# Casts of a pair's split on ScalarE instead of VectorE, and a reordered start, in a one-core recommendation tower

## What is computed

```python
e = stack([tbl_f[ids[:, f]] for f in range(39)], axis=1)      # x0: 512 x 39 x 16
xk = x0 = e
for W in (f0, f1, f2):                                         # 39*39, 128*39, 128*39 rows x 128
    z = einsum('bfd,bgd->bfgd', x0, xk).reshape(b, f * g, d)
    xk = einsum('bpd,pm->bmd', z, W);  outs.append(xk)
h = concatenate([concatenate(outs, 1).sum(-1), dense_ctx], 1)
h = maximum(h @ W_top1 + b1, 0);  h = maximum(h @ W_top2 + b2, 0);  y = h @ W_top3
```

## Time and profile before

| | |
|---|---|
| median of 3 runs | 708.94 us (708.28 to 708.96) |
| profiled execution: its own time | 706.03 us |
| its span, first to last instruction | 704.3 us |
| busy: PE, DVE, ACT, POOL | 96%, 88%, 71%, 36% of the span |
| chain that ended last | PE 60%, DVE 19%, issue 8%, ACT 3% |

### The profile page before, as it was taken

The page is one execution under the profiler, slowest core; times in us unless marked ns, Lnnn a source line. Parts: engine busy times, 40 slices in busy tenths (PEclk is TensorE's granted clock), DMA queues, the critical chain, the costliest instruction groups (busy, mean ns, idle before and its releaser), DMA issues.

```text
span 704.3 us, 11656 instructions
## 1 busy us (share of the span) xinstructions
PE 673.9 (96%) x3569; PEld 489.3 (69%) x3569; DVE 616.7 (88%) x1412; ACT 498.5 (71%) x1663; POOL 254.7 (36%) x247
## 2 busy tenths in 40 slices
PE   3787999999999999999999999999999999999998
PEld 0365677667777887767777778666776787777777
DVE  1579899999999877999999887899999887899991
ACT  3156678778786657878786657778787666787882
POOL 5674817148512707126710713406831000111020
PEclk9799999999999999999999999999999999999999
DMA  7630121203020210202111020110302020030000
GB/s 227 229 80 23 36 62 22 74 3 96 4 82 11 51 47 4 82 12 63 39 49 42 15 84 4 48 46 22 78 11 83 1 66 28 0 92 1 1 1 2
DMA packets 23411, 33.85 MB, mean 48 GB/s; under 512 B 7815, under 2 KB 10615, under 8 KB 22966
## 3 DMA queue, kind: packets, MB, share of 16 engines
q1 hardware_dynamic: 18230, 31.84, 14.7%
q0 software_dynamic: 5120, 1.29, 2.0%
HBM read 9.13 MB, written 0.00 MB: 13 GB/s over the span
## 4 chain that ended last, share of the span: by engine, by line
PE 60%; DVE 19%; issue 8%; ACT 3%; DMA 0%; SPq 0%; DVEq 0%
DVE sums L684 9%; PE x_ps L921 9%; PE v_ps L777 8%; PE v_ps L779 6%; PE v_ps L778 6%; PE a_ps L777 6%; PE a_ps L779 6%; PE a_ps L778 6%; PE s_ps L891 4%; PE s_ps L980 3%; ACT scaled L451 2%; DVE scaled L627 2%; DVE sums L673 1%; DVE scaled L617 1%; DVE z_sb L657 1%
## 5 line engine op out<-in xcount | busy, mean ns | idle before, releaser
L451 ACT ACTIVATE scaled<-a_ps,x0c 128x128 f32<-128x128 f32 x1216 | 350.3, 379 | 132.6 <-PE a_ps L779 125.7
L684 DVE SCALAR_TENSOR_TENSOR sums<-v_ps,x0c,sums 128x128 f32<-128x128 f32 x768 | 214.9, 340 | 33.3 <-PE v_ps L779 33.2
L777 PE MATMUL v_ps<-w_hi,x_hi 128*128 128x512 f32 x320 | 175.9, 550 | 8.5 <-DVE e_parts L573 4.5
L393 POOL DMA_INDIRECT e_sb<-in_tables,ids_now x140 | 165.5, 1182 | 41.1 <-issue 39.2
L409 POOL TENSOR_TENSOR diag_sb<-x0c,eye_sb 128x320 f32<-128x320 f32 x64 | 61.1, 955 | 316.4 <-PE s_ps L980 316.1
L779 PE MATMUL v_ps<-w_hi,x_lo 128*128 128x512 f32 x320 | 127.0, 397 | 0.0
L778 PE MATMUL v_ps<-w_lo,x_hi 128*128 128x512 f32 x320 | 126.5, 395 | 0.0
L777 PE MATMUL a_ps<-w_hi,x_hi 128*128 128x512 f32 (+1 forms) x320 | 124.2, 388 | 0.0
L779 PE MATMUL a_ps<-w_hi,x_lo 128*128 128x512 f32 (+1 forms) x320 | 123.1, 385 | 0.0
L778 PE MATMUL a_ps<-w_lo,x_hi 128*128 128x512 f32 (+1 forms) x320 | 123.1, 385 | 0.0
L921 PE MATMUL x_ps<-z_sb,w_sb 117*128 117x512 f32 (+1 forms) x210 | 108.0, 595 | 0.5 <-DVE z_sb L657 0.5
(11 more groups left out here) (112 smaller groups left out, 635.7 us busy)
## 6 DMA issues: line engine op xcount, KB each, us to landing
b_sb<-a_sb SPq DMA_DIRECT2D x300, 78.0 KB
w_sb<-in_w SPq DMA_DIRECT2D x1, 2496.0 KB
e_sb<-in_tables,ids_now POOLq DMA_INDIRECT x140, 2.6
s_sb<-in_w SPq DMA_DIRECT2D x2, 1024.0 KB, 5.1
wt_sb<-in_wt SPq DMA_DIRECT2D x1, 768.0 KB
s_sb<-in_w SPq DMA_DIRECT2D x1, 512.0 KB, 9.9
wt_sb<-in_wt SPq DMA_DIRECT2D x1, 512.0 KB
w_raw<-in_w0a SPq DMA_DIRECT2D x1, 409.5 KB
```

The costliest lines, as they stand in the source:

```text
L393: pool.indirect_dma_start(out=e_sb[0:rows, i, :], out_offset=None, in_=tables, in_offset=bass.IndirectOffsetOnAxis(ap=ids_now[0:rows, 0, i ...
L451: last = nc.scalar.activation(scaled[:, s % 2, to, j, :], bank[:, j * MAPS:(j + 1) * MAPS], ACT.Copy, scale=x0c[:, k % 4, s, lo + j:lo + j ...
L684: nc.vector.scalar_tensor_tensor(out=sums[:, s % 2, j, :], in0=v_ps[n % 2][:, j * MAPS:(j + 1) * MAPS], scalar=x0c[:, k % 4, s, lo + j:lo ...
L777: nc.tensor.matmul(to, high, w_high, start=True, stop=False)
```

## The change

- The two casts of a pair's split (pairs 1 to 7) go from DVE to ACT (`cast_pair`, at the head of ACT's half, at the first and third place of `split_at`); the two subtractions stay on DVE. Chunk 0's four places are 10, 11, 13, 14, where they were 11, 12, 13, 14.
- W1: its third piece is loaded ahead of W0 and all ids; the second piece is turned into four other banks; all three pieces are turned, rounded and subtracted ahead of x0.
- Filler matmuls of 512 columns (`warm_up`), 9, 1, 2 and 3 of them, stand around the turning of chunk 0's x0.
- Gathers: the second ten of the start no longer wait for `x0t`, and pair 1's are no longer paced.
- Chunk 1's first x0 is turned after the first half of chunk 0, and its rows of x0 after the third half; before, both stood ahead of chunk 0. Chunk 0's z0 places are (6, 8, 10, 11, 13, 14, 15), where they were (2, 4, 7, 9, 12, 14, 15), and its x0 turn stands at 16 and 18.
- The first group of each chunk waits for `x1_hi`, and only its third matmul for `x1_lo`; before, the group waited for `x1_lo` at its head.

```diff
-PACED_FROM, PACED_BY = 5, 0.6
+FIRST_TURN_AT, FIRST_A_AT = 0, 2
+FIRST_Z0_AT = (6, 8, 10, 11, 13, 14, 15)
+WARM_UPS = (9, 1, 2, 3)
-FIRST_SPLIT_AT = (11, 12, 13, 14)
-X0_TURN_AT = (15, 17)
+FIRST_SPLIT_AT = (10, 11, 13, 14)
+X0_TURN_AT, FIRST_X0_TURN_AT = (15, 17), (16, 18)
-        w1_banks = v_ps + a_ps
+        w1_banks = [v_ps + a_ps, [pair_ps, x1_ps, turn_ps, s_ps], v_ps + a_ps]
...
             for n in range(2):
-                if n == 1:
-                    pool.wait_ge(x0t_ready, 1)
                 for i in range(FQ):
...
-                if isinstance(pair, int) and pair == 1 and step > PACED_FROM:
-                    pool.wait_ge(v_done, 1 + int(PACED_BY * (step - 1 - PACED_FROM)))
...
+            def cast_pair(pair, step):
+                if step == 0:
+                    act.wait_ge(e_in, 16 * FH * pair)
+                    act.wait_ge(turned, 2 * pair)
+                    nc.scalar.activation(parts_of(e_parts, 0), e_sb[:, :, :].rearrange("p (u i) d -> p d u i", u=2),
+                                         ACT.Copy).then_inc(e_cast, 1)
+                if step == 2:
+                    act.wait_ge(e_left, pair)
+                    nc.scalar.activation(parts_of(e_parts, 1), e_rest[:, :, :].rearrange("p d (u i) -> p d u i", u=2),
+                                         ACT.Copy).then_inc(e_cast, 1)
...
             def split_pair(pair, step):
-                if step == 0:
-                    dve.wait_ge(e_in, 16 * FH * pair)
-                    dve.wait_ge(turned, 2 * pair)
-                split(step, ...)
+                if step == 1:
+                    dve.wait_ge(e_cast, 2 * pair - 1)
+                    nc.vector.tensor_tensor(rest, whole, parts_of(e_parts, 0), ALU.subtract).then_inc(e_left, 1)
+                if step == 3:
+                    dve.wait_ge(e_cast, 2 * pair)
+                    nc.vector.tensor_tensor(parts_of(e_parts, 2), rest, parts_of(e_parts, 1),
+                                            ALU.subtract).then_inc(e_split, 1)
...
             def first_pairs():
-                low_w1(1)
...
                 split_first(1)
-                low_w1(2)
...
+            def warm_up(n):
+                for _ in range(n):
+                    nc.tensor.matmul(x1_ps[:, :], sel_sb[:, IDB:IDB + 128], sel_sb[:, 0:COLS], start=True, stop=True)
...
+            for p in range(len(W1_PIECES)):
+                turn_w1(p)
             pe.wait_ge(consts_in, 32)
+            pe.wait_ge(w1_lo_ready, 8)
+            warm_up(WARM_UPS[0])
             turn_first(0)
+            warm_up(WARM_UPS[1])
...
                 nc.tensor.matmul(to, high, w_low, start=False, stop=False)
+                if low_ready:
+                    pe.wait_ge(x1_lo_ready, low_ready)
                 return nc.tensor.matmul(to, low, w_high, start=False, stop=True)
...
-                    if k == -1 and h == HALVES - 2:
-                        turn_first(1)
...
                         if h == 0:
-                            pe.wait_ge(x1_lo_ready, 4 * t + k + 1)
+                            pe.wait_ge(x1_hi_ready, 4 * t + k + 1)
...
+                    if 4 * t + k == 0 and h == FIRST_TURN_AT:
+                        turn_first(1)
+                    if 4 * t + k == 0 and h == FIRST_A_AT:
+                        pe.wait_ge(x0t_ready, 2)
+                        rows_of_x0(1)
...
+                warm_up(WARM_UPS[2])
                 pe.wait_ge(a_ready, 1)
                 for i in range(2):
                     select(i)
+                warm_up(WARM_UPS[3])
...
                     if i == T0 - 2:
-                        turn_w1(2)
+                        columns_of_x0(0)
```

More of the change, by code:

```diff
@@ L210, in dlrm_tower @@
         e_in = sem("e_in")
-        e_step = sem("e_step")
+        e_cast = sem("e_cast")
+        e_left = sem("e_left")
         e_split = sem("e_split")
@@ L506, in slot @@
                         nc.scalar.activation(x1_hi[:, (k + 1) % 2, :], x1_ps[:, :], ACT.Copy).then_inc(x1_hi_ready, 1)
-                    if k % 2 == 0 and k > -2 and h - 1 in X0_TURN_AT and exists(t, k + 2):
-                        part = X0_TURN_AT.index(h - 1)
+                    if k % 2 == 0 and k > -2 and h - 1 in x0_turn_at(t, k) and exists(t, k + 2):
+                        part = x0_turn_at(t, k).index(h - 1)
                         act.wait_ge(turned, 4 * t + k + 2 + part + 1)
@@ L581, in split_pair @@
             def split_pair(pair, step):
-                if step == 0:
-                    dve.wait_ge(e_in, 16 * FH * pair)
-                    dve.wait_ge(turned, 2 * pair)
-                split(step, e_sb[:, :, :].rearrange("p (u i) d -> p d u i", u=2),
-                      e_rest[:, :, :].rearrange("p d (u i) -> p d u i", u=2),
-                      lambda part: parts_of(e_parts, part), e_step, 3 * (pair - 1), e_split)
+                whole = e_sb[:, :, :].rearrange("p (u i) d -> p d u i", u=2)
+                rest = e_rest[:, :, :].rearrange("p d (u i) -> p d u i", u=2)
+                if step == 1:
[5 more added lines that the diff above has]
+                                            ALU.subtract).then_inc(e_split, 1)
             def low_w1(p):
@@ L601, in _ @@
             low_w1(0)
+            low_w1(1)
+            low_w1(2)
             dve.wait_ge(pads_ready, 4)
@@ L847, in last_block, with columns_of_x0, rows_of_x0 @@
                     mm.then_inc(y_done, 1)
+            def columns_of_x0(k):
+                for s in range(SUBS):
+                    mm = nc.tensor.matmul(turn_ps[:, F0 * s:F0 * (s + 1)], x0t[:, k % 4, 128 * s:128 * s + 128],
+                                          sel_sb[:, SEL_3:SEL_3 + F0], start=True, stop=True)
+                mm.then_inc(x0c_done, 1)
+            def rows_of_x0(k):
+                nc.tensor.matmul(pair_ps[0:3 * F0, :], sel_a, x0t[:, k % 4, :],
+                                 start=True, stop=True).then_inc(a_done, 1)
             def slot(t, k):
@@ L873, in slot @@
                             pe.wait_ge(y_ready, t)
-                        for s in range(SUBS):
-                            mm = nc.tensor.matmul(turn_ps[:, F0 * s:F0 * (s + 1)],
-                                                  x0t[:, (k + 1) % 4, 128 * s:128 * s + 128],
-                                                  sel_sb[:, SEL_3:SEL_3 + F0], start=True, stop=True)
-                        mm.then_inc(x0c_done, 1)
-                    if h == HALVES - 1 and exists(t, k + 2):
+                        columns_of_x0(k + 1)
+                    if h == HALVES - 1 and k != -1 and exists(t, k + 2):
                         pe.wait_ge(x0t_ready, x0t_events(t, k + 2))
@@ L882, in slot @@
                             pe.wait_ge(h2_ready, tile + 1)
-                        nc.tensor.matmul(pair_ps[0:3 * F0, :], sel_a, x0t[:, (k + 2) % 4, :],
-                                         start=True, stop=True).then_inc(a_done, 1)
+                        rows_of_x0(k + 2)
                     if step is not None and step in OUT2_AT:
@@ L908, in slot @@
                                 pe.wait_ge(macs, mac_count(at, last, 3))
-                        group(v_ps[n % 2], t, k, s, V_FIELDS[i]).then_inc(v_done, 1)
+                        group(v_ps[n % 2], t, k, s, V_FIELDS[i], 4 * t + k + 1 if h == 0 else None).then_inc(v_done, 1)
                         if not isinstance(t, int) or HALVES * 4 * t + n >= 2:
@@ L960, in slot @@
                     if turns_x0:
-                        part = X0_TURN_AT.index(h)
+                        part = x0_turn_at(t, k).index(h)
                         for d in range(D // 2):
```

69 lines of the change are left out of this document (38 added, 31 removed).

## The result

The changed kernel takes 701.99 us (median of 4 runs, 700.05 to 702.32) against 708.61 (4 runs, 707.78 to 708.96): a ratio of 0.9903, 95% interval 0.9882 to 0.9923. The forecast was 701.2. The profiled execution took 700.05 with a span of 698.0; before, 706.03 and 704.3.

A forecast was written before the change was run, and what follows sets the result against it. VectorE was taken to bound light and split chunks, TensorE the network's, and waits chunk 0. Start 5.2 and casts 2.5 off the profiled 706.03 gave 698.3, on the median 701.2 us; range 697.0 to 705.2.

The forecast's parts named there:

- the start: Chunk 0 up to chunk 1's start: earlier gathers and the start's other edits save 5.2 us, bounds 4.1 to 7.8.
- the casts: Later chunks: moving casts to ScalarE saves 2.5 us (0 to 3.5), 1.8 in split chunks, 0.7 in network chunks.
- The landing: Pair 1's last gather reaches its consumer in chunk 0 at 58.2 us, bounds 56.9 to 58.9; before, 62.19.
- a-part forecast at 59.8: TensorE's a-part of half 12, chunk 0, starts at 59.8, after the landing at 58.2, cast 0.45 and products 1.15.
- the fall of the clock: After TensorE idles some 5 us before half 12, one likely half-clock stretch moves chunk 1's start from 74.5 to 76.2.
- 14.7 and 1.7 for the clock: TensorE's work from half 12's a-part to chunk 1: 14.7 us at full clock, plus 1.7 for one half-clock stretch.
- the 74 to 77 forecast: A sign to look for: chunk 1 starts at 74 to 77 us, where before it started at 81.04.
- The edits costed at nothing: Start and later chunks: fillers, W1's order, removed pacing and the later x1_lo wait were each costed at nothing.
- the rival that the gathers don't come sooner: Start: DMA is busy with weights, pair 1 still lands at 62.2, only 0.8 + 2.5 won: 705.6 us; chance 0.08.
- the rival that ends slower: Every pair: e_left holds ScalarE at half 10, its late products hold TensorE's banks: 711 us; chance 0.06.
- the casts pay nothing: Split chunks: TensorE's list is nearly as long as VectorE's, so moving casts saves nothing: 703.7 us; chance 0.18.
- All pays: Whole kernel: gathers stay short, clock doesn't fall, casts pay in full, 7.8 + 3.5 = 11.3 us: 697.6; chance 0.18.

The follow-up runs named there:

- casts on VectorE: The changed kernel with all four operations of a pair's split back on VectorE, at the new places: 704.40 us, ratio 0.9954 to the kernel before.
- casts alone at 10: The kernel before with only the two casts moved to ScalarE and chunk 0's split at 10, 11, 13, 14: 704.01 us, ratio 0.9947.
- casts alone: The kernel before with only the two casts moved to ScalarE, chunk 0's split staying at 11, 12, 13, 14: 700.50 us, ratio 0.9905.
- the change at 11: The whole changed kernel with chunk 0's split at 11, 12, 13, 14 in place of 10, 11, 13, 14: 697.45 us, ratio 0.9861.
- The run with the gathers' wait put back: The changed kernel with the second ten gathers again waiting for chunk 0's x0t, pair 1 still unpaced: 706.31 us, ratio 0.9975.
- The kernel without fillers: The changed kernel without its 15 filler matmuls, split at 10, 11, 13, 14: 700.83 us, ratio 0.9909 to the kernel before.
- x0 turned at 15: The changed kernel with chunk 0's x0 turns at 15 and 17 in place of 16 and 18: 701.69 us, ratio 0.9907.
- the split three halves later: The changed kernel with chunk 0's split at 13, 14, 15, 16 and x0 turned at 17 and 18: 701.20 us, ratio 0.9886.
- the split two later: The changed kernel with chunk 0's split at 12, 13, 14, 15 in place of 10, 11, 13, 14: 697.86 us, ratio 0.9855.

## Why the prediction was right, and where it wasn't

The total was right to 0.8 us, the direction and the mechanism of the later chunks too. The terms were not all right: the start gave 2 us less than forecast, the casts 4 more in chunk 0, and their place there took 3 back, so that the total came so near is in part luck.

**By parts.** The runs form pairs that differ in one thing. In ratios times 708 us:

| part | from, to | us |
|---|---|---|
| start | before, casts on VectorE (0.9954) | -3.3 |
| start | casts alone at 10 (0.9947), the change (0.9903) | -3.1 |
| start | casts alone at 11 (0.9905), the change at 11 (0.9861) | -3.1 |
| casts, split at 11 | before, casts alone (0.9905) | -6.7 |
| split at 10 for 11 | casts alone (0.9905), at 10 (0.9947) | +3.0 |
| split at 10 for 11 | the change at 11 (0.9861), the change (0.9903) | +3.0 |

-3.1, -6.7 and +3.0 make -6.8, and 0.9903 is -6.9. Each ratio has an interval of about 0.2% to either side, so a single difference is known to some 2 us. Rows 2 and 3, and rows 5 and 6, come from the same four kernels: that they agree is one comparison, not two, and it says that start and place add to within some 3 us. The row from before to "casts on VectorE" holds the place 10 for VectorE's split as well, which was not tried apart.

**The start: forecast -5.2, measured -3.1 to -3.3.** This is the step that failed by size. The landing was right (58.2 forecast, 58.45 measured), and so was the wait of TensorE for products queued behind the cast (a-part forecast at 59.8, seen at 60.28), with the fall of the clock behind it. From the a-part to chunk 1 the forecast was 14.7 and 1.7 for the clock, 16.4; it took 18.2. 1.41 of the difference is the wait for `x0t` at half 19, which wasn't in the sum: the turn's two new places were listed as a change and not priced. The cast took 0.74, not 0.45, as its upper bound of 0.77 had it. So chunk 1 came at 78.49, outside the 74 to 77 forecast.

The run with the gathers' wait put back says where the term went. Against the change it prices the released gathers at 5.1 us (0.9975 and 0.9903), the whole of the forecast. Against the casts alone at 10 (0.9947), from which it differs only by the change's other edits, it is 2.0 slower, known to some 1.5: these edits, which the forecast costed at nothing or not at all, took some 2 us back. Its landing is also 2.3 later than in that kernel (64.12 and 61.79). Which of the edits did it is not shown; the wait for `x0t` above is one candidate, the gathers without pacing another.

**The casts: forecast -2.5, all in the later chunks.** There the size held: 0.65 in chunks 2, 6 and 10 (0.6 forecast); the network's chunks gave 0.06 and 0.10 in the change and 0.19 each in the casts alone (0.25 forecast); against the casts on VectorE with the rest of the change it is 0.18, 0.20 and, in chunk 12, 0.48. What the forecast left out is chunk 0: with the split at 11, letting ScalarE and not VectorE stand at the landing and cast is worth 4 us by itself (4.07 in the traces; by the ratios 6.7 less the 2.3 of the later chunks). With the split at 10 it is not: chunk 1 comes at 78.26 with the casts on VectorE and at 78.49 in the change. The forecast did not see it because it reckoned chunk 0 from the landing onward as the start's affair.

**The place of the cast at half 10, not priced by itself.** The forecast took the wait at half 12 as fixed by the landing, "whatever the start did before it". It is fixed only for that place of the cast. One half later the products of half 10 go ahead of the cast and TensorE doesn't wait there: 3.0 us. The wait that was left with the casts alone, 1.60, came one half later too.

**The edits costed at nothing.** Fillers: nothing, in two settings, since chunk 1's gathers land at 32.2 to 33.0 in every kernel that releases them, with fillers or without. That is also less than the forecast took for this landing: it was put as early as 30.3, 4.33 sooner, and came 1.67 sooner (32.99 for 34.66), although the gathers were issued 4.46 sooner. So the rival that the gathers don't come sooner held in part for the second ten, and not for pair 1. The pacing, W1's new order and the new places of chunk 0's z0 and turns were not undone by themselves, but for the turn of x0; they are within the start's 3.1 to 3.3. That W1's turning was not late is seen in the first group, which starts at 34.30, and its third matmul at 35.03, not 38.82. The later wait for `x1_lo`, the only edit beside the casts that touches the later chunks, seems to give 0.1 in most light chunks, which VectorE's full busy time was said to exclude, and to cost as much in the network's: chunk 4 takes 42.99 with the casts on VectorE against 42.87 before, and 42.81 in the change against 42.69 with the casts alone. It has not been undone alone. Nor did `e_left` hold ScalarE. Timelines of VectorE and ScalarE in chunk 6, as in the earlier trace rows:

```profile
297.65 0.70 DVE L623 TENSOR_TENSOR e_rest<-e_sb,e_parts 128x320 f32<-128x320 f32 x1
```

```profile
298.43 0.91 ACT L472 ACTIVATE scaled<-a_ps,x0c 128x128 f32<-128x128 f32 x3
299.18 0.51 ACT L507 ACTIVATE e_parts<-e_rest 128x320 bf16<-128x320 f32 x1
```

The subtraction had ended at 298.35, and the second cast follows the products with no gap: the rival that ends slower didn't occur. (Its price was summed wrongly: at six pairs, 1.5 us past its break-even of 3.5 adds 9 us and makes 718, not 711.) For pair 1, "the gathers don't come sooner" didn't occur either (landing 58.45), nor "the casts pay nothing" (0.65 each). "All pays" didn't, but the kernel with the split at 11 lands at its time, 697.45 against 697.6, by another way.

The Trainium skill says of ScalarE, VectorE and GpSimd that their "queues are strict FIFO" (PSUM — Partial Sum Buffer, "Engine vs sequencer instructions"). The traces agree, and in this case it is the rule that counts most: in the change the matmuls of half 10 had ended at 54.2, and ScalarE took up their products at 59.10, behind a cast that waited for a gather.

**What stays open.** That the change at 11 is better by 4.5 on the medians and by 3.0 in ratios is mostly the two groups of runs: the kernel before had 708.6 beside the change and 707.6 beside the other. Which stretches fall to half clock differs between executions (below), so a single trace doesn't tell the median of a wait that may or may not cost the clock.

## What to carry to other kernels

When an operation that waits for a late transfer is moved to another engine, ask first what stands behind it in that engine's order and who needs it: here the engine chosen was worth 4 us in one chunk with the same landing, and one step earlier in its list cost 3 us, both more than the 0.65 us that the move saved in each of three later chunks. Place the wait as late as the consumer of its result allows, and check the next consumer after that (here the split's end, then the copy of x0) for the wait that comes in its stead. A list of edits with one total wants runs that differ in one edit each; the total alone was forecast well from terms that were off by 2, 4 and 3 us.

## What was unexpected of the hardware

- Waits of about one length were followed by a fall of the granted clock or by none. The kernel without fillers waited 3.07 us at half 12 and the casts alone at 10 3.15, and both went on at the full clock; the change waited 3.17 and fell for 3.4 us; x0 turned at 15 waited 3.15 and fell for 6.8. In the second half of chunk 0, 1.81 was followed by 6.8 us at half clock with the split three halves later, and 2.05 by none with the split two later. One kernel differs too: the runs of the split three halves later are 3 to 5 us apart, at a mean of 0.998 and of 0.990. By the Trainium skill the array is throttled unless activity releases it (TensorE: Matmul & The Clock Gate, "What's actually happening"); the traces agree that falls follow waits of TensorE, but a wait of a given length did not always bring one.
- ScalarE's cast of 128x320 took 805 ns on the mean with the order of the elements rearranged on reading `e_sb`, and 509 from `e_rest`; VectorE took 429 and 315 for them.
- Indirect gathers issued back to back took 0.94 us each, and 1.06 to 1.94 in four of the last five of pair 1; before, the late ones took 1.26 and 1.66.
